# Four graph layers on one core: layers 0 and 1 of the next graph inside layer 3 of this one, and layer 3's tail inside the next layer 2

## The reference

```python
for each graph:                                    # B = 16, N = 1024, F = 64
    # layers 0 and 1 (slopes 0.2 and 0.1, layer 1 with a bias)
    h = x @ W
    e = leaky_relu((h @ a1)[:, None] + (h @ a2)[None, :])
    attn = softmax(where(adj > 0, e, -9e15), axis=-1)
    x = layernorm(x + elu(attn @ h + bias))
    # layer 2: eight heads, dot-product scores plus a bias by edge type
    s = leaky_relu(q_h @ k_h.T / 8 + edge_bias[adj, h], 0.2)
    x = layernorm(x + concat_h(softmax(where(adj > 0, s, -1e9)) @ v_h) @ Wp + bp)
    # layer 3: a sum over 64 features for every pair of nodes
    u, v = hp @ W1.T, hp @ W2.T                    # hp = x @ lin_w.T + lin_b
    e[i, j] = sum_f a[f] * leaky_relu(u[i, f] + v[j, f], 0.2)
    x = layernorm(x + elu(softmax(where(adj > 0, e, -9e15)) @ hp))
```

## Time and profile before

| | us |
|---|---|
| median of 3 runs | 9713.67 (9707.58 to 9726.64) |
| the profiled execution's own time | 9715.05 |
| its span, first to last instruction | 9713.2 |
| TensorE busy, weight loads apart | 8693.8 |
| VectorE busy | 7718.4 |
| ScalarE busy | 6774.4 |
| GpSimd busy | 1410.6 |
| mean granted TensorE clock | 0.972 |

### The profile page before, as it was taken

One profiled execution on the slowest core, in us unless ns is written; L12 is line 12 of the kernel. 1 busy time (PEld: TensorE's weight loads), 2 busy tenths in 40 slices (PEclk: granted clock), 3 DMA queues, 4 the chain that ended last, 5 costly groups with the idle time before them and its releaser, 6 DMA issues.

```text
span 9713.2 us, 176082 instructions
## 1 busy us (share of the span) xinstructions
PE 8693.8 (90%) x64203; PEld 4229.6 (44%) x64748; DVE 7718.4 (79%) x11658; ACT 6774.4 (70%) x7901; POOL 1410.6 (15%) x582
## 2 busy tenths in 40 slices
PE   6998989989899898998989989899898988989889
PEld 4435344453544535445354443544435444353443
DVE  6787977879788697886968779687796877968779
ACT  4776767768676686766867668676686766867667
POOL 1203012030120301103021020211202112021000
PEclk9999999999999999999999999999999999999999
DMA  2405023060230603306032060320604205042050
GB/s 74 99 9 137 8 64 88 9 144 1 70 83 9 144 1 76 77 9 144 1 85 68 9 143 1 90 63 9 144 1 95 57 13 140 2 103 50 16 119 2
DMA packets 1104730, 597.18 MB, mean 61 GB/s; under 512 B 103234, under 2 KB 1086274, under 8 KB 1103746
## 3 DMA queue, kind: packets, MB, share of 16 engines
q1 hardware_dynamic: 1103746, 584.54, 25.5%
HBM read 76.77 MB, written 4.19 MB: 8 GB/s over the span
## 4 chain that ended last, share of the span: by engine, by line
issue 59%; PE 16%; SPq 11%; DVE 5%; ACT 4%; DMA 3%; POOL 2%; DVEq 0%; ACTq 0%; POOLq 0%
SPq L328 11%; PE psum L477 4%; PE psum L435 3%; DMA work<-work 3%; ACT work L728 2%; DVE work L1020 2%; PE psum L674 2%; PE psum L431 2%; DVE work L989 1%; PE psum L522 1%; PE psum L443 1%; POOL rstd L1279 1%; ACT work L739 1%; PE psum L514 1%; PE psum L453 1%
## 5 line engine op out<-in xcount | busy, mean ns | idle before, releaser
L888 ACT ACTIVATE work<-vw,ucol 128x1024 f32<-128x1024 f32 x3072 | 3310.0, 1140 | 475.9 <-PE psum L674 474.0
L674 PE MATMUL psum<-work,pick 128*32 128x512 f32 x32768 | 3623.5, 594 | 12.1 <-ACT work L888 12.1
L1206 DVE TENSOR_SCALAR work<-vw,ucol 128x1024 f32<-128x1024 f32 x5120 | 3440.8, 746 | 203.2 <-ACT ucol L868 116.2
L989 DVE CUSTOM_DVE_ANT_0 work<-psum,work 128x1024 f32<-128x1024 f32 x1284 | 1551.3, 1209 | 1009.6 <-ACT work L728 962.8
L674 PEld LDWEIGHTS psum<-work,pick 128*32 128x32 f32 x32768 | 1012.8, 110 | 2325.3 <-issue 2202.2
L728 ACT ACTIVATE work<-psum,beta 128x1024 f32<-128x1024 f32 x1024 | 1138.3, 1112 | 913.9 <-PE psum L435 910.4
L739 ACT ACTIVATE work<-work,least 128x1024 f32<-128x1024 f32 x1282 | 1467.4, 1145 | 43.5 <-DVE least L989 42.7
L477 PE MATMUL psum<-work,vw 128*64 128x256 f32 x8192 | 1105.8, 419 | 403.9 <-DMA work<-work 403.7
L1020 DVE STREAM_TRANSPOSE work<-work 128x1024 f32<-128x1024 f32 x960 | 1190.5, 1240 | 40.0 <-DMA work<-work 38.9
L477 PEld LDWEIGHTS psum<-work,vw 128*64 128x64 f32 x8192 | 617.0, 148 | 841.7 <-issue 364.6
L431 PE MATMUL psum<-mask,ident_b 128*128 128x512 bf16 x2231 | 734.5, 400 | 261.5 <-DVE least L989 164.6
(11 more groups left out here) (132 smaller groups left out, 6231.7 us busy)
## 6 DMA issues: line engine op xcount, KB each, us to landing
work<-work SPq DMA_DIRECT2D x3840, 128.0 KB, 2.4
adj_in<-in_adj SPq DMA_DIRECT2D x128, 512.0 KB, 3.6
x_in<-in_x SPq DMA_DIRECT2D x17, 256.0 KB, 3.2
xT_in<-in_xT SPq DMA_DIRECT2D x17, 256.0 KB, 4.5
out<-yout SPq DMA_DIRECT2D x16, 256.0 KB, 2.8
work<-in_WqT SPq DMA_DIRECT2D x1, 128.0 KB
work<-in_WkT SPq DMA_DIRECT2D x1, 128.0 KB
work<-in_WvT SPq DMA_DIRECT2D x1, 128.0 KB
```

The source lines that it names most:

```text
L674: mm = pe.matmul(slot[32 * q:32 * q + 32, cols], pick[:, 15 - kk:47 - kk], ring[kk % 4][q][:, cols], start=False, stop=(kk == 15), skip_gr ...
L888: ins = act.activation(ring[kk % 4][q], v3, ACT.Relu, bias=col)
L989: dve.tensor_tensor_reduce(probs[n % 4], score[n % 2], probs[n % 4], -ALPHA[layer], 3.0e38, ALU.add, ALU.min, least[:, n % 4:n % 4 + 1]).t ...
L1206: ins = dve.tensor_scalar(ring[kk % 4][q], v3, col, 0.0, ALU.add, ALU.max)
```

## The change

The work inside a layer stays; its place in time changes, and so do the ways of turning tiles.

- **Layers 0 and 1 of graph g+1 lie inside the ring of graph g.** After each group u of the ring every engine calls `ahead(g + 1, it, u)`. With v = u - 63 * layer: TensorE makes the scores of tile m after groups v = 4m, ScalarE its first pass after 4m+1, VectorE the least value after 4m+2, ScalarE the exponential after 4m+3, VectorE the block transposes after 4m+4. Output, norm and the next layer's column and values lie at v = 43 to 62. All of it uses the one PSUM buffer `turn` and one buffer `probsA`.
- **Their tiles are turned by pairs through DMA**, as layer 2 turns quads: two tiles are transposed by blocks into `blocksA` (which is the buffer `adj_in`), 16 DMAs move them to `pairA_T`, and `pv_pair` multiplies at v = 17, 25, 33, 41. There is one buffer of each.
- **Layer 3's tiles are turned singly in the same way** (`blocks3`, `tile3T`, 16 DMAs), except the last, which TensorE transposes. `pv_tile` follows at kk = 14 of the next tile.
- SyncE's queue takes the moves in a fixed order: pairs 0, 1, tile 0, pairs 2, 3, tiles 1, 2, 3, pairs 4, 5, tile 4, pairs 6, 7, tiles 5, 6, then one DMA of 2 MB that copies the mask.
- **Layer 3's tail lies in the next layer 2**: the last exponential before its first pass, the last product, output, norm and final scaling in its steps 0 to 4, the store behind the third quad.
- ScalarE takes 5 units of 12 in three groups in place of 3 of 8 (`act_units`).
- The first graph's layers 0 and 1 run through the same 128 steps without a ring; the last graph's ring has nothing beside it. Before the ring TensorE makes the next graph's column and values, then 24 fillers, then turns x.

The diff, cut to its core:

```diff
+def act_units(u, ahead):
+    if ahead:
+        return (3,) if u % 3 == 1 else (2, 3)
+    return (3,) if u % 2 else (2, 3)
...
+            def move(dst, src, done):
+                for turn_ in range(4):
+                    for a in range(4):
+                        c = (a + turn_) % 4
+                        sp.dma_start(dst[32 * c:32 * c + 32, :, a, :], src[32 * a:32 * a + 32, :, c, :]).then_inc(done, 16)
...
+            def move_pair(g, m):
+                ready(s_blocks_a, g * 2 * NT + 2 * m + 2)
+                if m or not_first(g):
+                    ready(s_pv_a, g * NT + m)
+                move(pairA_T.rearrange("p (b c x) -> p b c x", c=4, x=F),
+                     blocksA.rearrange("p (b c x) -> p b c x", c=4, x=F), s_moved_a)
+            def move_tile(g, T):
+                ready(s_blocks3, g * (NT - 1) + T + 1)
+                if T:
+                    ready(s_pv3, g * NT + T)
+                move(tile3T.rearrange("p (b c x) -> p b c x", c=4, x=32),
+                     blocks3.rearrange("p (b c x) -> p b c x", c=4, x=32), s_moved3)
...
+            def ahead(g, it, u):                      # TensorE
+                layer, v = divmod(u, SPAN)            # SPAN = 63
+                if layer < 2:
+                    if v % 4 == 0 and v < 4 * NT:
+                        scores_a(g, it, layer * NT + v // 4)
+                    if v in (17, 25, 33, 41):
+                        pv_pair(g, layer * NT // 2 + (v - 17) // 8)
+                    if v == 44:
+                        turn_out_a(g, it, layer)
+                    if v == 53:
+                        turn_x_a(g, it, layer)
...
+            def layer3(g, it, more):                  # TensorE
+                if more:
+                    column(g + 1, it, 0)
+                    values_a(g + 1, it, 0)
+                pe.wait_ge(s_leaky, g * TILES2 + TILES2 - 1)
+                for i in range(KEEP):                 # KEEP = 24
+                    pe.matmul(score[0][:, 0:HALF], ident_b[:], mask[:, 0, 0:HALF], start=True, stop=True)
+                both_ready(ONE + it[1] + it[0][("xT2", 0)], s_xn2, g * 2 + 2)
+                turned(turn_rows(lambda t: x2[:, t, :], F))
...
+            def relu_a(g, it, m):                     # ScalarE
+                if m or not_first(g):
+                    act.wait_ge(s_blocks_a, g * 2 * NT + m)
+                filled(act, it, ("a", m))
...
+            def blocks_a(g, m):                       # VectorE
+                if m % 2 == 0 and (m or not_first(g)):
+                    dve.wait_ge(s_moved_a, (g * NT + m // 2) * 256)
+                dve.wait_ge(s_probs_a, g * 2 * NT + m + 1)
+                dst = blocksA.rearrange("p (b t i) -> p b t i", t=2, i=32)
+                dve.transpose(dst[:, :, m % 2, :], probsA.rearrange("p (b j) -> p b j", j=32))\
+                   .then_inc(s_blocks_a, 1)
...
+            def layer3(g, it, more):                  # VectorE
...
+                norm(acc[:], zb[:], s_var2)
+                if more:
+                    column_low(it, 0, g + 1)
+                dve.wait_ge(s_rstd2, g + 1)
+                scaled_to((x2[:],), zb[:], s_xn2)
```

1408 lines of the change are left out of this document (744 added, 664 removed).

## The result

The changed kernel takes 10508.55 us (median of 4 runs, 10494.58 to 10521.8), the kernel before 9720.15 (9707.58 to 9730.25): 1.0812 of it, with a 95% interval of 1.0789 to 1.0834. The forecast was 10,009, in the right direction and 500 us short. The profiled execution took 10518.66 us, its span is 10516.9, and TensorE's mean granted clock fell from 0.972 to 0.908.

A forecast was written before the change was run, and what follows sets the result against it. Moves by DMA through one buffer were taken to bound the ring. A period of 361 + 2.5 + 227.5 + 23 = 614 us gave 530 + 15 x 614 + 269 = 10,009; range 9700 to 10,300 (ring 340 to 380).

The forecast's parts named there:

- Bound and mechanism: In the ring: single buffers for a pair make moves, VectorE and TensorE a closed loop; ring 361 us.
- The price of a move: SP's queue: 16 DMAs at about 0.65 us an issue, then landing; 12.4 us a move, 8.4 as lower bound.
- The idle times foreseen: VectorE's transposes of layers 0 and 1 wait for DMA: some 9 us at pairs 1, 2, 5, up to 12 at 4, 6.
- The loop: Ring, from one pair's landing to the next: VectorE 12.6, TensorE's group and product, move 12.4; 28.8 us for eight groups.
- full on TensorE: Ring stretches without waits for moves, summed as TensorE's work: 34 groups between layers (58 us), last 36 groups (62), plus other matmuls.
- a cold start: TensorE in the ring at low clock after dry spells: 3 us charged twice, the loops hiding the rest.
- if the engines, as full as they are, lose another 5% to each other: Upper bound for the ring with its step to layer 2's values: 380 us against 361.
- Rival B: Ring's tile stretches: TensorE's clock stays low, a loop of eight groups takes 33.6 us against 28.8; 10,370 us; chance 0.11.
- The gap: Between layer 2 and the ring: values wait for VectorE behind the norm, fillers come onto the path; 8 us later, 23.
- Layer 2 and the ends: Layer 2 grows by 5.5 us for layer 3's tail; first ring starts at 530, last ring and tail take 269.
- A: Rival for the ring: shorter dry spells make the change pay, needing a ring of 341 at 23; 9497 us; chance 0.20.
- C: Rival for the moves: small rows need double engine time, a move about 20 us; 11,075 us; chance 0.07.

The follow-up runs named there:

- half the issues: Changed kernel with 8 DMAs instead of 16 per move in layers 0, 1 and 3, half their blocks not moved; 9865.27 us, 1.0157 of the kernel before.
- two block buffers: Changed kernel with a second buffer for a pair's blocks and layer 3's buffers placed elsewhere; 9700.1 us, 0.9993 of the kernel before.
- zero fill: Changed kernel with four groups' worth of zero-weight matmuls before the ring groups that wait for a landed move; 10585.59 us, 1.0898 of the kernel before.
- warm gap: Kernel with two block buffers, column and values behind v3, norm ahead of the loop's turn, 24 fillers before turning x and 10 behind; 9602.32 us, 0.9890.
- thin tail: Kernel with two block buffers, the second half of layer 3's norm done on one tile of eight in layer 2; 9662.59 us, 0.9945 of the kernel before.
- norm first: Kernel with two block buffers, layer 2's two sums and norm put ahead of the loop's turn; 9681.29 us, 0.9965 of the kernel before.

## Why the forecast came out short

The measured columns are two graphs of the changed kernel: the second, as above, where TensorE came to the ring at half clock as in 12 of 15 graphs, and the third, where it came at full clock.

| term of one period | forecast | second graph | third graph |
|---|---|---|---|
| pair 0 landed, after the first unit | 37 | 42.4 | 36.9 |
| pair 1, pair 2 | 66, 96 | 72.6, 102.2 | 67.6, 97.4 |
| the wait of pair 4 | 216 | 231.4 | 226.6 |
| pair 5, pair 6 | 244, 275 | 263.7, 295.3 | 258.4, 289.8 |
| end of the ring | 361 | 388.4 | 383.1 |
| to layer 2's first pass | 2.5 | 2.5 | |
| layer 2 to the last division | 227.5 | 228.4 | 230.8 with the row above |
| gap ahead of the ring; behind the graph | 23 | 29.6; 27.4 | 27.4; 29.3 |
| period, from first unit to first unit | 614 | 646.7 | 643.2 |
| start of the first ring; last ring and tail | 530; 269 | 538; 270 | |

A period lasts 647.3 us in the mean. Its excess of 33.3 us over the forecast is 26.6 in the ring, 1.5 in layer 2 and its first pass, and 5.2 in the gap. With the ends, 15 x 33.3 + 8 + 1 = 508 makes 10,517, the profiled span.

**Bound and mechanism: right.** The ring is bounded by moves through one buffer, and both experiments on that loop took the time out (643 us with half the issues, 808 with two block buffers). The price of a move was right: 16 issues in 10.4 us and 2.1 us to land are 12.5, forecast 12.4. SyncE's timeline and the issues of the changed kernel:

```profile
1262.50 10.40 SPq L376 DMA_DIRECT2D work<-work  x16
1274.49 10.39 SPq L376 DMA_DIRECT2D pairA_T<-adj_in  x16
```

```profile
work<-work SPq DMA_DIRECT2D x3840, 128.0 KB, 2.4
pairA_T<-adj_in SPq DMA_DIRECT2D x2048, 64.0 KB, 2.1
...
work<-work SPq DMA_DIRECT2D x1792, 32.0 KB, 1.9
```

The idle times foreseen (some 9 us at pairs 1, 2 and 5, up to 12 at 4 and 6) are 9.4, 10.1, 9.9, 13.0 and 12.8. The loop was 28.8 in the forecast, with 30 and 31 where a tile stands between, and is 30.2, 29.6, 32.3 and 31.6; these four cost 6 us of the 27. From the landing at 1226.5 to the pair's product at 1241.9 are 15.4 us where the sum had 14.4; the rest is the product and the move.

**The step that failed: "full on TensorE".** The stretches without a wait for a move were summed as TensorE's work, with 3 us to get going and 3 for a cold start: 120 us from pair 2's landing to the wait of pair 4, and 86 at the end. They measured 129.2 and 93.1 (129.2 and 93.3 in the third graph), some 16 of the ring's 26.6 us. The first of the two divides into 87.3 us to the first scores of layer 1, where the forecast had 78, and 41.9, where it had 42. So the miss lies in the 34 groups between the layers and in the last 36:

```profile
1286.40:1373.70 87.30, 81.87 (x684) 27.74 (x684) 78.52 (x127) 69.43 (x71) 2.10 (x1) 0.93 0.14 25
1479.40:1572.50 93.10, 85.62 (x721) 30.17 (x722) 77.02 (x127) 70.64 (x72) 2.09 (x1) 0.97 0.27 63
```

TensorE is busy for 81.9 and 85.6 us, where groups, products, matmuls and a cold start were summed to 75 and 83, and idle for 5.4 and 7.5, where 3 was allowed. Its busy time and its waits were both put too low (ends of records count as busy here too). Two of the waits are for VectorE's units, which stand behind output and norm of layer 0 (1324.7 to 1336.5) and behind the output of layer 1:

```profile
1338.76 5.77 PE L793 MATMUL psum<-work,pick 128*32 128x512 f32 x36 [2.51 <-DVE work L1356]
...
1524.65 1.93 PE L793 MATMUL psum<-work,pick 128*32 128x512 f32 x16 [1.90 <-DVE work L1356]
```

I had summed the engines and let the fullest set the time. Where one engine's work stands in its queue ahead of its ring units, the others wait although all three have work. The kernels with two block buffers show this for the chain of scores, first pass, least value, exponential and transposes (25 us of waits on ScalarE, 28 on VectorE, and 16.5 us of the ring gone with the scores one group earlier). In the changed kernel that edit takes 2 us off the stretch between the layers and nothing off the end. So this chain is shown as the cause of 2 of the 16 us; what the rest is made of no run takes apart. The forecast had named such a term and used it only for its upper bound ("if the engines, as full as they are, lose another 5% to each other", 380).

**TensorE's clock: charged in the wrong place.** The forecast charged 3 us for a cold start after pairs 2 and 6. It charged nothing for the clock with which TensorE comes to the ring, and this is the second miss, some 4 of the 26.6 us. In the same execution the last microseconds of the gap and the time to pair 0's landing were, in the second graph (low clock, and landed at 42.4) and in the third (high clock, and landed at 36.9, as forecast):

```profile
1178.60:1184.10 5.50, 5.50 (x14) 3.07 (x13) 0.00 (x0) 2.48 (x3) 0.00 (x0) 0.50 0.00 0
1184.10:1221.00 36.90, 32.13 (x201) 9.95 (x204) 26.53 (x38) 27.09 (x29) 0.00 (x0) 0.85 0.07 15
```

```profile
1825.80:1830.80 5.00, 5.00 (x24) 3.09 (x23) 0.00 (x0) 2.48 (x3) 0.00 (x0) 1.00 0.00 0
1830.84:1867.70 36.86, 29.95 (x226) 8.15 (x229) 28.37 (x40) 32.29 (x34) 0.00 (x0) 1.00 0.14 30
```

In the loops the clock is 0.82 to 0.90, and it costs nothing there (zero fill). Rival B fell: it had a loop of 33.6 us set by TensorE, and the loops are 29.6 to 32.3. The four waits of the loops are together 5.7 us above the forecast.

**The gap.** Forecast 23, measured 29.6 and 27.4 ahead of the second and third rings. Foreseen were the column's low part behind the norm and the fillers on the path, and both are there. Not foreseen was that the loop over the graphs now turns here: ahead of the sum VectorE stands idle for 2.03 us and TensorE for 3.31 ahead of the column, released by nothing, where the sum followed after 0.1 us before. So TensorE comes cold to the fillers: 24 take 7.38 us, where 31 took 6.85 and the forecast had 5.3. The first 10 or 11 run at a granted clock of 0.50, the rest at 1.00, so they do bring the clock up. It fell again in the 8 matmuls with G, after the transposes and 1.20 us of idleness: they take 5.68 us. In the third graph, behind the same 1.20 us, the clock stayed up and they take 3.67. What decides between the two isn't shown. With fillers behind the transposes as well (warm gap) they take 3.60. In the changed kernel's timeline:

```profile
1157.78 1.42 DVE L1341 TENSOR_TENSOR za<-za,heads_T 128x512 f32<-128x512 f32 x2 [2.03 <-issue]
1157.80 3.67 PE L523 MATMUL psum<-xT_in,WD 64*128 64x512 f32 x4 [3.31 <-issue]
...
1167.45 7.38 PE L764 MATMUL psum<-mask,ident_b 128*128 128x512 bf16 x24
...
1176.90 5.68 PE L523 MATMUL psum<-xTa,G 65*128 65x512 f32 x8 [1.20 <-ACT xTa L994]
...
1825.62 3.67 PE L523 MATMUL psum<-xTa,G 65*128 65x512 f32 x8 [1.20 <-ACT xTa L994]
```

**Layer 2 and the ends: right.** +6.4 us where 5.5 were charged for the tail, and the thin tail shows for the 2.7 us that it takes away that they are paid in full. The first ring was 8 us later than said, the end 1 us longer.

**The rivals.** A asked for a ring shortened by faster issues or by the engines' four groups of advance, and neither is there; only two block buffers bring the ring under its 341 us. C is refuted: rows of 256 and 128 bytes land in 2.1 and 1.9 us, faster than those of 512 in 2.4. The Trainium skill, "DMA: Bandwidth & Descriptors", Specifications, wants 512 bytes at least and warns of a read-modify-write below them; the landings from SBUF to SBUF here, of fewer bytes as well, don't bear out a higher price at these sizes.

**The range.** It ended at 380 for the ring, and the ring was 383 to 389: three errors of the same sign, the full stretches, the loops and the clock ahead of the ring, met, and the gap's came on top. The range had an end for the first and none for the others.

## What to carry to other kernels

When work is interleaved with a full ring, find the one buffer whose hand-over passes through the slowest step and give it a second copy before judging the idea: here one wait made the difference between 8% slower and no slower. Where several engines are full, a sum of their work is too low a forecast, and a producer placed one group earlier in its queue can be worth more than any work removed (248 us for seven tiles' scores a layer, made one group earlier). Look where a loop turns, for its idle time comes to lie on the path. And look at more than one period: two lengths in one execution were TensorE's clock here, and a comparison of single periods would have taken them for an effect.

## What the runs showed of the hardware

- A DMA of 32 partitions cost SyncE about 0.65 us to issue, whatever it carried: 16 take 10.40 us for a tile of layer 3 and 10.39 for a pair with twice the bytes. The price of a transposition by 16 DMAs was mostly their number.
- At the turn of the hardware loop in the gap VectorE stood idle for 2.0 to 3.3 us and TensorE for 2.6 to 3.4, in all the kernels whose gap was read. For VectorE the idle time moved with the turn (norm first). The Trainium skill, "Advanced Engine Details and Errata", Control Flow Timing, gives a branch some 51 ns, one with a comparison some 108; "Runtime: NRT & Kernel Launch", Instruction fetch mechanics, says that a taken branch out of the prefetched window has to fetch its target first. The idle times are far above the first page's figures and would fit such a fetch, though no run here separates the fetch from the rest of the turn.
- The same instructions in the same execution met the ring at one of two clocks: 0.50 in the changed kernel in 12 graphs of 15, 1.00 in 3. It cost about 5.6 us of the ring behind and 2 of the gap ahead.
- A higher granted clock and a longer time can go together (0.932 and 10,586 us against 0.908 and 10,509): the clock by itself is no measure of what a kernel loses.
